# Moving the first heads' operands within SBUF, spreading maxima, and pausing between indirect DMAs in a two-layer attention and mixture-of-experts kernel

## The chip, the cores and the metric

The kernel runs on one core of a Trainium2 chip. Times are device microseconds of one launch. The engines are TensorE (PE, matmuls into the eight PSUM banks `ps`), VectorE (DVE), ScalarE (ACT), GpSimd (POOL) and SyncE (SP, which only issues DMAs). Engines wait for each other through counting semaphores; a DMA adds 16 to one when it has landed. Lower is better.

## The reference

Input `x` has 32 x 32 positions (N = 1024 tokens) and C = 384 channels; there are 12 heads of 32 channels. Everything is float32.

```python
x = x + conv_attention(group_norm(x))        # layer 1: 12 heads, scores + rel_h + rel_w, softmax, projection
t = tokens(x)
t = t + attention(layer_norm(t))             # layer 2: q k^T / sqrt(384), softmax, projection
t = t + moe(layer_norm(t))                   # gate: top 2 of 8 experts, normalized weights
# moe, for each expert e and its tokens:
#   y_e = relu(x @ w1[e].T + b1[e]) @ w2[e].T + b2[e]      hidden size 1536
#   out += weight[token, e] * y_e
```

## The kernel before

In the code L = 0 is layer 1 and L = 1 is layer 2. In layer 2 every factor of the query and key products is split into a high part, which TensorE's fp32r form holds exactly, and a low rest. A product is then three: high by high, low by high, high by low.

**Query and key products.** Six products u = 0 to 5 (queries and keys of three groups of four heads, in turn). Each has two halves of 512 tokens, of nine matmuls each (line 712). u writes the PSUM banks 0 and 1 or 2 and 3 in turn. ScalarE copies each to SBUF (line 1224), and VectorE splits it into the tile `parts`: a high part (line 1019) and a low part (line 1021).

**The way of the operands.** `parts` holds a head's 32 channels on 32 partitions. The later products want three or four blocks of 32 rows one under the other in `qa` and `ka` (97 rows, for the scores) and `qm` and `km` (96 rows, for the maxima). SyncE stores the parts of four heads into the DRAM tensor `heads` (`store_qk`, line 425, eight DMAs of 256 KB for each group), waits until they have landed, and loads `qm` and `km` (`load_m`, lines 437 and 438) and `qa` and `ka` (`load_a`, lines 444 to 447) of head 0 and head 1 (`first_heads`). Then it stores the other two groups, waits again, and loads head 2's. Later heads are loaded one by one.

**Maxima and scores.** For a head's softmax the maximum of each query's scores is needed first. `max_scores` (line 730) makes two matmuls of 96 rows and 512 columns for a query tile, which go round the PSUM banks 0, 1 and 7 (`RING`, `max_bank`). VectorE reduces each to one column (`maximum`, line 1039). A matmul waits until the bank that it writes has been reduced. When eight tiles are through, TensorE turns the column of maxima into a row (`turn_max`, line 735). ScalarE copies it, stores it to DRAM (line 1267) and, when that has landed, loads it as the 97th row of `qa` (line 1273), so that the score product (line 745) already subtracts it. ScalarE takes the exponential (line 1252), `out_product` (line 755) multiplies by the values, and GpSimd adds the first tiles of the sums (lines 597 and 601).

The order of TensorE's work is written out. `BETWEEN[1]` says which (head, query tile) maxima stand at each of the eight value product tiles (line 817): thirteen in all. Where a list has two, the first stands behind the first third. `TURN[1]` says at which value tile ScalarE copies head 0's row; until it has loaded it, it evicts no value tile. Inside `head`, step s makes the scores of key tile s, then maxima of the next head or the one after (`MAXIMA_FIRST` for head 0: head 1's tiles 5, 6 and 7, then head 2's), then output products at s = 1, 3, 5 and 7.

**Routing and experts.** VectorE works out for each token its two experts and the row of `xs` where its normalized row (`tn`) goes. GpSimd scatters them with 16 indirect DMAs of 128 rows, one for each of the two choices r and eight token tiles (line 653). TensorE makes the first tile of 128 rows itself, by 48 products with one-hot matrices (line 915), so that it needs no scatter. SyncE waits for all 16 scatters and loads the second tile (line 532); ScalarE loads the later ones. ScalarE copies each turned tile from PSUM to `xT` (`turned`, line 1325). Ahead of the first it issues two DMAs that spread the rows' places over the partitions, `where<-where` and `where_row<-where` (lines 1328 and 1330), for VectorE's compare (line 1171).

Each row tile then runs 72 products (line 930), ScalarE's relu (line 1343), VectorE's split (lines 1183 and 1185), and 36 split products (line 942). Before the ninth of the twelve hidden groups TensorE turns the next row tile (`turn`, line 908). GpSimd splits the next expert's second weight (`split_expert`, lines 559 and 561).

**The end.** Results of the rows that went to a token's first expert lie in `low`. When SyncE signals (`y_all` at 1) that the tiles of all but the last expert are stored, GpSimd gathers them with eight indirect DMAs (line 663), waits for all eight, multiplies each by the token's weight (line 669) and adds it to `t` (line 672). When the tiles up to the last but one are stored (`y_all` at 2) it gathers the second choice. TensorE and VectorE add the last tile's rows.

## Time and profile before

| | us |
|---|---|
| median of 3 timed runs | 922.0 (921.08 to 925.76) |
| the profiled execution | 930.64 |
| span of that execution | 928.8 |
| TensorE busy | 871.1 (94%) |
| VectorE busy | 486.7 (52%) |
| GpSimd busy | 510.6 (55%) |
| ScalarE busy | 333.0 (36%) |
| mean granted clock of TensorE | 0.97 |

The span is the time from the first to the last instruction of the profiled execution; 1.84 us of its time lie outside. Times of rows are microseconds from the span's start. A busy share of TensorE is no measure of its pace: matmuls are pipelined, and their ends are modelled. Idle time counts where the engine is on the chain that ended last. The granted clock is a share of full speed: 1.00 is 2.4 GHz, 0.50 is 1.2 GHz.

### The profile page before, as it was taken

The numbers are of one execution on the slowest core, as the hardware profiler recorded it, in microseconds if no ns is written. First come the engines' busy times: TensorE is split into PE (matmuls) and PEld (weight loads), VectorE is DVE, ScalarE is ACT, GpSimd is POOL, SyncE is SP. The second block draws the span as 40 slices with busy tenths as digits, with TensorE's granted clock in tenths as the row PEclk, the third lists the DMA queues.
The fourth block names the chain that finished last, engine by engine and source line by source line (L and its number), as shares of the span: only waits on it lengthen the run. The fifth ranks groups of instructions, "written<-read, shape, count | busy, mean of one in ns | idle before, by whom it ended". The sixth has DMA issues, their size and how long they took to land.

```text
span 928.8 us, 18189 instructions
## 1 busy us (share of the span) xinstructions
PE 871.1 (94%) x6200; PEld 662.8 (71%) x6201; DVE 486.7 (52%) x869; ACT 333.0 (36%) x582; POOL 510.6 (55%) x436
## 2 busy tenths in 40 slices
PE   4998999999999889899999998659999999999998
PEld 3475566666665467555555554459999999999997
DVE  5344866776773466677877833624233242233234
ACT  0131254554555222355555662203222232222311
POOL 0300287777875670357676761778357168087383
PEclk9999699999999999799999998769999999999999
DMA  9498523534425009636564426551752644545225
GB/s 300 106 225 257 181 81 94 162 88 118 137 67 167 12 6 227 153 116 196 169 215 145 150 72 206 185 207 35 264 196 93 242 162 148 181 164 189 72 67 158
DMA packets 75073, 139.68 MB, mean 150 GB/s; under 512 B 11576, under 2 KB 49656, under 8 KB 75024
## 3 DMA queue, kind: packets, MB, share of 16 engines
q1 hardware_dynamic: 63424, 120.72, 42.2%
q10 hardware_dynamic: 9552, 12.07, 3.9%
q0 software_dynamic: 2048, 6.29, 2.1%
q8 instruction: 25, 0.41, 0.2%
q14 instruction: 24, 0.20, 0.1%
HBM read 91.82 MB, written 43.55 MB: 146 GB/s over the span
## 4 chain that ended last, share of the span: by engine, by line
PE 83%; DVE 6%; SPq 3%; issue 3%; DMA 2%; ACT 1%; another core or an unknown queue 1%; POOL 1%; ACTq 0%; DVEq 0%; POOLq 0%
PE ps L930 18%; PE ps L755 14%; PE ps L942 13%; PE ps L745 11%; PE ps L730 10%; PE ps L747 5%; PE ps L702 4%; SPq L425 2%; PE ps L861 2%; PE ps L839 2%; DVE mhalf L1039 2%; DMA heads<-parts 1%; PE ps L915 1%; PE ps L817 1%; DMA km<-heads 1%
## 5 line engine op out<-in xcount | busy, mean ns | idle before, releaser
L1039 DVE TENSOR_REDUCE mhalf<-ps 128x1 f32<-128x512 f32 x384 | 240.7, 676 | 92.9 <-PE ps L730 90.9
L1252 ACT ACTIVATE prob<-ps 128x1024 f32<-128x1024 f32 x192 | 192.4, 1025 | 151.8 <-PE ps L747 87.3
L601 POOL TENSOR_TENSOR qf<-qf,prob 128x1024 f32<-128x1024 f32 x76 | 181.3, 2386 | 41.1 <-ACT prob L1252 31.7
L930 PE MATMUL ps<-xT,w 128*128 128x128 f32 x1440 | 166.2, 277 | 8.0 <-issue 6.7
L930 PEld LDWEIGHTS ps<-xT,w 128*128 128x128 f32 x1440 | 165.4, 194 | 8.5 <-issue 8.5
L745 PE MATMUL ps<-qa,ka 97*128 97x512 f32 x384 | 148.1, 429 | 2.9 <-ACT prob L1252 2.0
L730 PE MATMUL ps<-km,qm 96*128 96x512 f32 x384 | 139.1, 440 | 8.6 <-DMA km<-heads 4.5
L1343 ACT ACTIVATE h_f<-ps,b1c 128x128 f32<-128x128 f32 x240 | 68.5, 369 | 148.2 <-PE ps L930 113.7
L559 POOL TENSOR_SCALAR w_hi<-w_raw 128x384 fp32r<-128x384 f32 x96 | 56.1, 584 | 105.2 <-DMA w_raw<-in_w 105.1
L730 PEld LDWEIGHTS ps<-km,qm 96*128 96x128 f32 x384 | 75.2, 197 | 50.9 <-DVE mhalf L1039 31.3
L561 POOL TENSOR_TENSOR w_lo<-w_raw,w_hi 128x384 fp32r<-128x384 f32 x96 | 101.8, 1060 | 8.0
L745 PEld LDWEIGHTS ps<-qa,ka 97*128 97x128 f32 x384 | 69.2, 193 | 49.9 <-issue 19.0
L755 PE MATMUL ps<-prob,va 128*32 128x256 f32 x1536 | 104.1, 386 | 0.0
L597 POOL TENSOR_TENSOR qf<-prob 128x1024 f32<-128x1024 f32 x24 | 57.0, 2376 | 74.9 <-ACT prob L1252 74.9
L1183 DVE CAST h_hi<-h_f 128x512 fp32r<-128x512 f32 x60 | 32.8, 546 | 123.0 <-ACT h_f L1343 119.0
L942 PE MATMUL ps<-w_hi,h_hi 128*128 128x384 f32 x240 | 83.8, 349 | 0.0
L942 PE MATMUL ps<-w_hi,h_lo 128*128 128x384 f32 x240 | 80.5, 336 | 0.0
L942 PE MATMUL ps<-w_lo,h_hi 128*128 128x384 f32 x240 | 80.3, 334 | 0.0
L747 PE MATMUL ps<-qb,eb 128*128 128x512 f32 x192 | 76.9, 401 | 0.0
L755 PEld LDWEIGHTS ps<-prob,va 128*32 128x32 f32 x1536 | 42.8, 110 | 42.6 <-issue 16.7
L1049 DVE RECIPROCAL rec<-vsb 128x64 f32<-128x64 f32 x96 | 49.8, 534 | 42.9 <-ACT vsb L1278 42.9
L618 POOL COPY va<-vf 128x256 f32 (+1 forms) x24 | 9.6, 398 | 96.4 <-DVE vf L1025 56.2
(171 smaller groups left out, 957.7 us busy)
## 6 DMA issues: line engine op xcount, KB each, us to landing
w<-in_w SPq DMA_DIRECT2D x24, 768.0 KB, 7.3
w_raw<-in_w SPq DMA_DIRECT2D x24, 768.0 KB, 11.2
heads<-parts SPq DMA_DIRECT2D x60, 256.0 KB, 4.7
qa<-heads SPq DMA_DIRECT2D x24, 256.0 KB, 3.5
ka<-heads SPq DMA_DIRECT2D x24, 256.0 KB, 3.5
qb<-heads SPq DMA_DIRECT2D x12, 512.0 KB, 5.4
xs<-zero SPq DMA_DIRECT2D x8, 768.0 KB, 4.5
qm<-heads SPq DMA_DIRECT2D x12, 384.0 KB, 5.0
```

The costliest lines, as they stand in the source:

```text
L561: pool.tensor_tensor(w2_lo[b][:, c, :], w2_raw[b][:, c, :], f(w2_hi[b][:, c, :]), ALU.subtract).then_inc(w2_ok[b], 1)
L597: pool.tensor_tensor(acc[b], prob[:, 0, :], prob[:, 1, :], ALU.add).then_inc(a_ok[L], 1)
L601: pool.tensor_tensor(acc[b], acc[b], prob[:, n % NP, :], ALU.add).then_inc(a_ok[L], 1)
L730: mm(max_bank(qt, half), qm[b][0:96, qt * P:(qt + 1) * P], km[b][0:96, half * HALF:(half + 1) * HALF], start=True, stop=True).then_inc(sm_ ...
L745: last = mm(out, ka[b][0:97, s * P:(s + 1) * P], qa[b][0:97, cols], start=True, stop=(L == 1))
L747: last = mm(out, eb[:, s * P:(s + 1) * P], qb[b][:, cols], start=False, stop=True)
L755: last = mm(ps[HD * r:HD * (r + 1), 6, half * QUARTER:(half + 1) * QUARTER], lhs, src[:, r * QUARTER:(r + 1) * QUARTER], start=start, stop ...
L930: last = mm(ps[:, g, c % HG * P:(c % HG + 1) * P], w1[b][:, k, c * P:(c + 1) * P], xT[:, k, :], start=(k == 0), stop=(k == KT - 1))
L942: last = mm(ps[:, 6, 0:C], h[:, c, :], w[:, c, :], start=(c == 0 and n == 0), stop=(c == HC - 1 and n == 2))
L1039: v.tensor_reduce(mhalf[:, b, qt, half:half + 1], max_bank(qt, half), AX.X, ALU.max).then_inc(mx_ok[L], 1)
L1252: act.activation(prob[:, s % NP, :], ps[:, 2 + 2 * (s % 2):4 + 2 * (s % 2), :].rearrange("p a b -> p (a b)"), ACT.Exp).then_inc(p_ok[L], 1)
L1343: last = act.activation(h_f[:, c, :], ps[:, g, c % HG * P:(c % HG + 1) * P], ACT.Relu, bias=b1c[b][:, c:c + 1])
```

## The change

1. *Layer 2, operands.* `qm` and `km` of the first two heads are copied straight from `parts` by DMAs within SBUF (`direct`), four of 128 KB, as soon as u = 0 and 1 are split, ahead of the stores. Behind the first group's stores follow `qa` and `ka`: twelve more, in place of the loads from DRAM. The stores stay. Head 2's `qm` and `km` are loaded behind the second group's stores and not behind the third's.
2. *Layer 2, maxima.* Head 0's query tiles 0 to 3 go among the query and key products (`AMONG`): behind u = 3, behind the first half of u = 4, and behind each half of u = 5. VectorE reduces tiles 0 and 1 behind the split of u = 3, tile 2 behind that of u = 4, tile 3 behind that of u = 5 (`REDUCED`). The products therefore use the banks 2 to 5 in place of 0 to 3 (`qk_bank`), and the value products start at bank 6 (`v_bank`). `BETWEEN[1]` has nine tiles left, and `TURN[1]` goes from value tile 5 to 4.
3. *Routing.* GpSimd waits between the scatters of the two choices until ScalarE has copied the first `xT`. The two DMAs of `where` go from ScalarE's queue to SyncE's.
4. *The end.* Two gathers of the first choice are issued; then, for each tile, GpSimd waits for its gather, multiplies, adds, and issues the gather after next.

```diff
-           ([(0, 0), (0, 1)], [(0, 2)], [(0, 3), (0, 4)], [(0, 5)], [(0, 6), (0, 7)], [(1, 0)], [(1, 1), (1, 2)], [(1, 3), (1, 4)]))
-TURN = (7, 5)
+           ([(0, 4)], [(0, 5)], [(0, 6)], [(0, 7)], [(1, 0)], [(1, 1)], [(1, 2)], [(1, 3), (1, 4)]))
+TURN = (7, 4)
+AMONG = {(3, 1): 0, (4, 0): 1, (5, 0): 2, (5, 1): 3}
+REDUCED = {3: (0, 1), 4: (2,), 5: (3,)}
...
+        def qk_bank(L, u):
+
+            return 2 * L + 2 * (u % 2)
+
+        def v_bank(L, tt):
+
+            return 4 + (tt + 2 * L) % 3
...
+                def direct(h, dst, at, done):
+
+                    sp.dma_start(f(dst), f(parts[h * HD:(h + 1) * HD, 0, at, :])).then_inc(done, 16)
+
+                if L == 1:
+                    sp.wait_ge(split[1], 4)
+                    for h in range(2):
+                        direct(h, qm[h][0:HD, :], 1, ld_m[1][h])
+                        direct(h, km[h][0:HD, :], 2, ld_m[1][h])
                 for m in range(KT):
                     store_qk(m)
                     if m == 0 and L == 1:
+                        for h in range(2):
+                            for i, at in enumerate((0, 1, 1)):
+                                direct(h, qa[h][i * HD:(i + 1) * HD, :], at, ld_a[1][h] if i < 2 else ld_d[h])
+                            for i, at in enumerate((2, 2, 3)):
+                                direct(h, ka[h][i * HD:(i + 1) * HD, :], at, ld_a[1][h] if i < 2 else ld_d[h])
+                    if m == 1 and L == 1:
                         sp.wait_ge(st_q[1][0], 16 * 8)
-                        first_heads()
+                        load_m(2, 0)
...
-            sp.wait_ge(route_ok, 2)
+            sp.wait_ge(route_ok, 3)
+            sp.dma_start(where_dram.rearrange("(p t) -> p t", p=P), where[:, 1, :]).then_inc(ld_l, 16)
+            sp.wait_ge(ld_l, 16)
+            sp.dma_start(where_row[:], where_dram.partition_broadcast(P)).then_inc(ld_l, 16)
             sp.wait_ge(scattered, 16 * 2 * TT)
...
             for r in range(2):
+                if r == 1:
+                    pool.wait_ge(x_ok, 1)
                 for tt in range(TT):
...
+            pool.wait_ge(y_all, 1)
+            for tt in range(2):
+                gather(0, low_dram, where_i[:, 0, tt:tt + 1], tt, gathered[0][tt])
+            for tt in range(TT):
+                pool.wait_ge(gathered[0][tt % 2], 16 * (tt // 2 + 1))
+                pool.tensor_tensor(gy[0][:, tt, :], gy[0][:, tt, :], wts[:, 0, tt:tt + 1].broadcast_to([P, C]), ALU.mult).then_inc(early_ok, 1)
+                pool.wait_ge(early_ok, 2 * tt + 1)
+                pool.tensor_tensor(t[:, tt, :], t[:, tt, :], gy[0][:, tt, :], ALU.add).then_inc(early_ok, 1)
+                if tt + 2 < TT:
+                    gather(0, low_dram, where_i[:, 0, tt + 2:tt + 3], tt + 2, gathered[0][tt % 2])
+            pool.wait_ge(y_all, 2)
+            for tt in range(TT):
+                gather(1, ys_dram, where_g[:, tt:tt + 1], tt, gathered[1][tt])
...
+                        if half == 1:
+                            last.then_inc(qk_mm[L], 1)
+                        if L == 1 and (u, half) in AMONG:
+                            if u == 3:
+                                pe.wait_ge(wide_ok, 4)
+                            max_scores(0, 0, AMONG[u, half])
...
                     v.scalar_tensor_tensor(lo, src, s, f(hi), ALU.mult, ALU.subtract).then_inc(split[L], 1)
+                    for qt in REDUCED.get(u, ()) if L == 1 else ():
+                        maximum(0, 0, qt)
...
-            act.wait_ge(route_ok, 3)
-            act.dma_start(where_dram.rearrange("(p t) -> p t", p=P), where[:, 1, :]).then_inc(ld_l, 16)
-            act.wait_ge(ld_l, 16)
-            act.dma_start(where_row[:], where_dram.partition_broadcast(P)).then_inc(ld_l, 16)
             turned(0)
```

Beside this the value products of layer 2 wait at tile 1 until all six products have been copied, since they share banks 4 and 5; head 0's and head 1's first scores wait for `ld_d` too; and the first choice's gathers have semaphores of their own.

## Rows read from the trace of the kernel before

**Rows 1.** The chain of work that ended last, share of the span by engine.
```profile
PE 83%; DVE 6%; SPq 3%; issue 3%; DMA 2%; ACT 1%; another core or an unknown queue 1%; POOL 1%; ACTq 0%; DVEq 0%; POOLq 0%
```

**Rows 2.** Timeline, TensorE, layer 2's start: start, us, line, operation, tiles, [idle before <-releaser].
```profile
350.47 0.84 PE L712 MATMUL ps<-x_hi,parts 128*128 128x512 f32 x3
...
361.19 0.70 PE L730 MATMUL ps<-km,qm 96*128 96x512 f32 x2 [1.88 <-DMA km<-heads]
...
374.70 0.28 PE L735 MATMUL ps<-ident,mcol 128*8 128x128 f32 x1
...
381.47 0.70 PE L745 MATMUL ps<-qa,ka 97*128 97x512 f32 x2 [0.86 <-DMA qa<-row]
...
388.64 1.22 PE L730 MATMUL ps<-km,qm 96*128 96x512 f32 x2 [2.29 <-DMA km<-heads]
...
393.58 0.75 PE L745 MATMUL ps<-qa,ka 97*128 97x512 f32 x2
```

**Rows 3.** Windows: length, busy PE, PEld, DVE, ACT, POOL, granted clock, DMA share, GB/s.
```profile
383.00:389.00 6.00, 3.52 (x8) 2.32 (x9) 3.38 (x7) 2.27 (x3) 2.74 (x2) 0.54 0.57 145
389.00:394.00 5.00, 5.00 (x25) 2.41 (x25) 2.58 (x4) 1.29 (x2) 4.07 (x2) 0.53 0.01 2
```

**Rows 4.** Timeline, SyncE's queue, layer 2's start.
```profile
346.82 7.89 SPq L425 DMA_DIRECT2D heads<-parts  x8
...
385.44 0.33 SPq L437 DMA_DIRECT2D qm<-heads  x1
```

**Rows 5.** Timeline, TensorE, routing and first row tile.
```profile
606.77 8.14 PE L915 MATMUL ps<-hot,tn 128*128 128x128 f32 x48 [4.97 <-DVEq L1156]
621.59 10.29 PE L930 MATMUL ps<-xT,w 128*128 128x128 f32 x72 [6.67 <-issue]
...
635.88 0.49 PE L908 MATMUL ps<-ident,xs 128*128 128x128 f32 x3
```

**Rows 6.** Timeline, TensorE, last expert.
```profile
884.63 0.49 PE L908 MATMUL ps<-ident,xs 128*128 128x128 f32 x3
...
888.55 8.30 PE L930 MATMUL ps<-xT,w 128*128 128x128 f32 x72 [1.32 <-ACT xT L1325]
```

**Rows 7.** Timeline, ScalarE, routing and last expert.
```profile
620.86 0.49 ACT L1325 ACTIVATE xT<-ps 128x384 f32<-128x384 f32 x1 [24.17 <-remote]
...
887.83 0.49 ACT L1325 ACTIVATE xT<-ps 128x384 f32<-128x384 f32 x1 [5.41 <-remote]
```

**Rows 8.** Timeline, GpSimd, the seventh and the last of the 16 scatters.
```profile
612.95 1.50 POOL L653 DMA_INDIRECT xs<-tn,where_i  x1 [0.30 <-issue]
...
624.89 0.96 POOL L653 DMA_INDIRECT xs<-tn,where_i  x1 [0.31 <-issue]
```

**Rows 9.** Timeline, GpSimd, last expert: last gather, products, sums, first later gather.
```profile
885.28 0.95 POOL L663 DMA_INDIRECT gy<-low,where_i  x1 [0.30 <-issue]
888.44 6.95 POOL L669 TENSOR_TENSOR gy<-gy,wts 128x384 f32<-128x384 f32 x8 [2.22 <-DMA gy<-low,where_i]
895.47 9.65 POOL L672 TENSOR_TENSOR t<-t,gy 128x384 f32<-128x384 f32 x8
906.94 0.99 POOL L663 DMA_INDIRECT tn<-ys,where_g  x1 [1.82 <-SPq L544]
```

**Rows 10.** DMA issues: tiles, engine, count, KB each, median us to landing.
```profile
xnT<-osb SPq DMA_DIRECT2D x92, 32.0 KB, 1.8
...
km<-eb SPq DMA_DIRECT2D x2, 256.0 KB, 4.8
```

**Rows 11.** Timeline, VectorE, layer 2's start.
```profile
352.46 1.22 DVE L1021 SCALAR_TENSOR_TENSOR parts<-prob,parts 128x1024 fp32r<-128x1024 f32 x1
...
361.75 1.28 DVE L1039 TENSOR_REDUCE mhalf<-ps 128x1 f32<-128x512 f32 x2
```

**Rows 12.** Timeline, SyncE's queue, routing.
```profile
628.18 0.33 SPq L532 DMA_DIRECT2D xs<-xs  x1
```

**Rows 13.** Timeline, VectorE, routing.
```profile
613.17 1.16 DVE L1171 TENSOR_SCALAR hot_last<-where_row,last_slot 128x1024 f32<-128x1024 f32 x1 [3.95 <-DMA where_row<-where]
```

More of the change, by code:

```diff
@@ L308, in build_program @@
         zero_st = sem("zero_st")
+        ld_d = [sem(f"ld_d{i}") for i in range(2)]
         early_ok = sem("early_ok")
@@ L326, in build_program @@
         y_all = sem("y_all")
-        gathered = [[sem("gathered0")] * TT, [sem(f"gathered1{i}") for i in range(TT)]]
+        gathered = [[sem(f"gathered0{i}") for i in L2], [sem(f"gathered1{i}") for i in range(TT)]]
         t_out = sem("t_out")
@@ L816, in values @@
                         for k, (x, w) in enumerate(third):
-                            last = mm(ps[:, 4 + tt % 3, 0:C], x, w, start=(n == 0 and k == 0),
+                            last = mm(ps[:, v_bank(L, tt), 0:C], x, w, start=(n == 0 and k == 0),
                                       stop=(n == 2 and k == len(third) - 1))
@@ L1013, in _, with maximum @@
                     v.wait_ge(st_r[1], 16 * (NH - 2))
+                def maximum(h, b, qt):
+                    for half in range(2):
+                        v.wait_ge(sm_ok[L], 2 * (TT * h + qt) + half + 1)
+                        v.tensor_reduce(mhalf[:, b, qt, half:half + 1], max_bank(qt, half), AX.X, ALU.max).then_inc(mx_ok[L], 1)
+                    if qt == TT - 1:
+                        v.wait_ge(mx_ok[L], 2 * TT * (h + 1))
+                        wait(v, mT_ok[L], h - 1)
+                        v.tensor_reduce(mcol[:, b, :], mhalf[:, b], AX.X, ALU.max).then_inc(mc_ok[L], 1)
                 for u in range(2 * KT):
```

89 lines of the change are left out of this document (36 added, 53 removed).

## The prediction

> **What bounds the kernel now.** I read the chain of work that ended last first: TensorE (PE) holds 83% of it, VectorE (DVE) 6%, the issue of SyncE's DMAs 3% [rows 1]. So the time is the work of TensorE plus the places where it stands, and a change that removes no product can win only those places and what TensorE's clock loses beside them. I went through TensorE's timeline for them in the three stretches that the diff touches: the start of layer 2's attention, the routing, and the last expert.
>
> *Layer 2.* Between 350.47 and 381.47 TensorE runs the last query and key products, then the value products with thirteen query tiles of maxima between them. It stands 1.88 us before the first maximum, for `km<-heads`, and 0.86 us before the first score of head 0, for the row of negated maxima. Inside head 0 it stands 2.29 us at 388.64, again for `km<-heads` [rows 2]. The granted clock is 0.54 in 383 to 389 and 0.53 in 389 to 394 [rows 3], that is 1.2 GHz for most of it; the engine had been short of work since 380.6 [rows 2]. The operands come late because SyncE's queue first stores 2 MB to DRAM (8 issues, 7.89 us), waits until they land, and loads them back; head 2's load stands behind 16 more stores and is issued at 385.44 [rows 4].
>
> *Routing.* The 48 gathering products end at 614.91 (606.77 + 8.14), and the first expert product starts at 621.59, 6.67 us later; the 72 products then take 10.29 us [rows 5], where a later tile takes 8.30 [rows 6]. ScalarE's copy `xT<-ps`, which needs nothing but the end of those 48 products, starts at 620.86 [rows 7], 5.9 us after it. In that time GpSimd issues 16 scatters one after the other, until 625.85 [rows 8].
>
> *Last expert.* The same sign again: the three transposes at 884.63 end near 885.1, the copy that needs them starts at 887.83 [rows 6, 7], 2.7 us later, and TensorE stands 1.32 us [rows 6], while GpSimd issues eight gathers (the last one 885.28 to 886.23) [rows 9]. I read both as one thing: what TensorE signals arrives late while GpSimd issues indirect DMAs back to back. The trace shows the delay, not its cause.
>
> **The change part by part.** *Layer 2, the maxima between the query and key products.* Eight matmuls (tiles 0 to 3) move from the value products to behind u = 3, 4 and 5; none is added. 39 products run from 350.47 to 359.31 (361.19 less 1.88), 0.227 us each, so half a product of nine is 2.04 [rows 2]. Tile 0 needs head 0's `qm` and `km` by 350.5. They are issued at 346.8 and 347.2, when the first two splits are done. Copies within SBUF took 1.8 us (32 KB) and 4.8 us (256 KB) to landing [rows 10]; 128 KB between them, 3.3, gives 350.5, in time or up to 1.5 late, and lateness here only eats into the next wait. That wait is new: VectorE's splitting of u = 3 ends at 353.70 (352.46 + 1.22), and a reduction takes 0.64 (1.28 for two) [rows 11]. TensorE is through with tile 0 and half of u = 4 at 352.97, and tile 1's two matmuls reuse banks that come free at 354.34 and 355.0: it stands 1.4 and 0.4. Queued behind it is the other half of u = 4, and so ScalarE's copy and VectorE's split of it. The products then end at 358.63 + 1.84 (eight matmuls) + 1.8 = 362.3. Tile 3 is reduced only after u = 5 is split (about 365.0 to 366.3), so tile 4's second matmul, behind the first value tile, waits to 365.65: 1.6 more. Value tiles 0 to 4 (45 products of 384 columns for 512, 0.17 each, 7.7 us), ten maxima matmuls (2.3) and the wait bring head 0's column to its turn at 374.0, against 374.70 [rows 2]. From turn to first score it took 6.77 us (row stored, loaded back) [rows 2]; TensorE's own remaining work (27 value products 4.6, eight maxima 1.8, the turn 0.2) is as long: 380.8. By the same durations the work from 361.19 to 380.61 before (69 value products, 26 maxima, the turn) would be 17.9, and it took 19.4, so small waits of up to 1.5 come on top. I take 381.5, the start of before: the 1.88 and 0.86 removed return as waits for VectorE, and nothing is won up to here. Setting `TURN` to value tile 4 blocks ScalarE, with value tile 5's eviction behind it, for the row's store; value tile 7 needs only tile 4 evicted, so this costs nothing.
>
> *Layer 2, SyncE's queue.* It gets 16 copies of 128 KB (0.35 to 0.6 each to issue) for 12 loads with 2 MB, so no fewer bytes; but the wait for the landing of the first stores goes. Eight stores pass in 7.89 us [rows 4], 256 KB per us. From 346.8: 0.5 MB copied, 2 MB stored, 1.5 MB copied, 2 MB stored is 6 MB or 24 to 26 us, and head 2's `qm` and `km` are issued near 372, when head 0's maxima are done, ten microseconds before they are needed. If copies whose source is 32 partitions run at half that pace it is 380, still in time. The 2.29 us wait goes whole. What holds TensorE then is VectorE: at 380.8 it has eight reductions of 0.64 left (head 1's tiles 4 to 7) and the short one of the column, so head 2's first maximum ends and the turn of head 1 follows at 386.1; two scores, two maxima and 16 output products (1.9 in all) put the fifth score of head 0 at 388.2, or 388.9 from a start at 381.5. Before it is 393.58 [rows 2]. That is 4.7, if TensorE keeps 2.4 GHz. In the record the clock falls just after 383, when the engine has stood 0.86 us before the first score and is being paced by VectorE; the same stretch is somewhat fuller now, but 353 to 356 and 364 to 367 are emptier. With the fall where it was, only the wait is won: 2.3. Bounds 1.0 (a start at 382.8 and that fall) and 6.0 (at 380.8, and VectorE less in the way); I take 4.7, near the upper end, since most of what was lost there is the wait and the low clock behind it.
>
> *Scatters in halves.* GpSimd issues eight scatters, to 615.71 (612.95 + 1.50, a gap of 0.30, 0.96) [rows 8], and then waits for the copy `xT`. If the late signal comes when issuing stops, or 1.5 us after it (887.83 against 886.23 [rows 7, 9]), `xT` starts at 615.8 to 617.3 and the expert products at 616.5 to 618.0 for 621.59: 3.6 to 5.1. Not all of it stays. The second half now runs from 617.5 to 627.5 (for 625.85), the row tile of the second 128 tokens, issued at 628.18 [rows 12] 2.3 us behind the last scatter, lands at 632.2 or so, and its transposes, at 635.88 before [rows 5], need it: 3.7 is the most that is left. And the clock may be at 1.2 GHz for the first products as now (2.0 us of the 10.29), or the second half may hold the signals of the first tile. Bounds 0 and 4.9; I take 3.0. GpSimd's weight splitting behind the scatters starts 2 us later; expert 1, whose weights it splits, comes two row tiles of some 15 us later. The two DMAs of `where` go from ScalarE's queue to SyncE's, behind expert 1's weights; VectorE's compare, which waits for them, stands at 613.17 [rows 13], and the next that needs VectorE is the first tile's cast behind the first expert products. Nothing, unless they come over 8 us late.
>
> This same compare shows something else: the scatter beside it took 1.50, its neighbours 0.96 [rows 8, 13]. The Trainium skill, "SBUF — State Buffer", section "SBUF: two separate sides", says that GpSimd cannot write an indirect DMA's descriptors while VectorE runs certain two-port operations, so that such a DMA waits for VectorE. This speaks against the change, since the second half now lies beside the first tile's three casts and subtractions. By it the last scatters, and the second row tile behind them, would come some 1.5 us later and the routing would win 1.5 to 2.
>
> *Gathers in turn.* Eight gathers, eight products (6.95) and eight sums (9.65), at 886.2, 895.4 and 905.1 by their ends, become two gathers, then product, sum, gather eight times: 0.87 + 1.21 + 1.25 = 3.3 each for six and 2.1 for two, from about 880.0: to 904.2. The next gathers may start at 906.94 [rows 9], so that 2.7 us cover it; each such microsecond beyond would fall on the end. Never more than two gathers stand in a row before the transposes at 884.63, so the 1.32 us wait goes: 1.3 (0 if a signal is late even behind one gather; 2.0 if the following tile's start is freed as well). The last burst of eight stays as it is.
>
> **The sum.** 4.7 + 3.0 + 1.3 = 9.0. The profiled execution took 930.64 with a span of 928.8, so 921.6 for a like one; the median of the timed runs is 922.0, 8.6 less than the profiled one, and gives **913.0**.
>
> **Rivals.** (1) *The clock takes part of it back, or was not lost in the timed runs.* A second fall of ten microseconds at 1.2 GHz, at the new waits at 353 or 364, costs 5.0: 918.0. If the timed runs of before don't fall at 383 at all (they are 8.6 below the profiled one, which speaks for it), layer 2 wins 1 to 2: 916.2. Against it: the stretch that fell is now fuller. (2) *The second half of the scatters holds the first tile's signals*: the second group of hidden values is signalled at 629.0 (627.5 and 1.5) and TensorE stands in the output products; routing wins nothing: 916.0. For it: a signal is late in both bursts [rows 7]; against: the late ones came after seven and eight issues without a pause, and the first tile's first groups end sooner behind it. (3) *The change does not do what it says*: copies within SBUF, all with source and target on the same 32 partitions, crawl, head 0 waits for `qa`, and layer 2 wins nothing: 917.7. (4) *Slower.* The new waits for VectorE at 353 to 355 and 364 to 366 lower the clock inside the products, where TensorE alone sets the pace, and it stays low to the start of the heads. 38 us at 1.2 GHz cost 19: 922.0 - 9.0 + 19 = 932.0. It decides from 18 us at the low clock on, where half of them passes the gain. Against it: 1.88 us of standing at 359.3 did not lower it [rows 2].
>
> **How the numbers follow.** My forecast 0.50, (1) 0.24, (2) 0.12, (3) 0.06, (4) 0.08. What a measurement of this kernel can tell from no change is some 0.5%, 4.6 us: faster is below 917.4. The forecast, (2) and most of (1) lie there: 0.77; the rest of (1) and (3) within: 0.15; (4) slower: 0.08. The range takes in the low ends of the bounds (6.0 + 4.9 + 2.0 = 12.9, with two more for run to run) and the cases (1) to (3): 907 to 918.5.
>
> **What would show it.** Right: no wait for `km<-heads` in layer 2, waits of 1.4 and 1.6 us for VectorE's reductions between and behind the query and key products, head 0's first score as far from the first product as before and the fifth 4.7 us nearer; `xT` within 2.5 us of the 48 products' end; no idle before the second last tile of the last expert. Wrong: a low granted clock between 350 and 380; expert products that wait in the first tile; sums of GpSimd that end behind the last row tile's store.

## The result and the profile after

| | before | after |
|---|---|---|
| median of 21 timed runs each, us | 924.39 (921.08 to 930.63) | 918.95 (915.79 to 923.66) |
| ratio, 95% interval | | 0.9938 [0.9922, 0.9953] |
| the profiled execution | 930.64 | 921.23 |
| its span | 928.8 | 919.4 |
| mean granted clock of TensorE in it | 0.969 | 0.976 |

The forecast was 913.0, with a range of 907.0 to 918.5. From profile to profile the span fell by 9.4 us, and the sum had said 9.0; but the medians fell by 5.4. The two differ because the profiled execution of before is one of its slowest (four of its 21 runs took 928.7 or more). What that execution had in excess was read as a property of the kernel. Two single runs of the experiments below, one of before_again (2944.28 us) and one of layer2_only (4746.78 us), are far outside all others and are left out of every figure.

The chain that ended last, by engine, is still TensorE's, for [rows 1]:

```profile
PE 85%; DVE 6%; DMA 3%; POOL 2%; issue 2%; ACT 1%; SPq 0%; ACTq 0%; DVEq 0%; POOLq 0%
```

**Layer 2.** Timeline of TensorE, after, for [rows 2] (start, us, line, operation, tiles, idle time before and what ended it). L742 is the maxima, L776 the turn, L788 the scores:

```profile
352.06 0.63 PE L742 MATMUL ps<-km,qm 96*128 96x512 f32 x2
355.92 1.10 PE L742 MATMUL ps<-km,qm 96*128 96x512 f32 x2 [1.15 <-DVE mhalf L1059]
...
367.38 0.50 PE L742 MATMUL ps<-km,qm 96*128 96x512 f32 x1 [1.45 <-DVE mhalf L1059]
...
375.90 0.28 PE L776 MATMUL ps<-ident,mcol 128*8 128x128 f32 x1
...
382.95 0.73 PE L788 MATMUL ps<-qa,ka 97*128 97x512 f32 x2
...
390.51 0.73 PE L788 MATMUL ps<-qa,ka 97*128 97x512 f32 x2
```

352.06 is the place of 350.47 in [rows 2]. From there the first score is 30.89 us away (31.00 before) and the fifth 38.45 (43.11). No wait for `km<-heads` is left, and the two new waits for VectorE are 1.15 and 1.45. The windows at the place of [rows 3] show that the clock no longer falls (columns as there):

```profile
385.00:391.00 6.00, 5.57 (x32) 2.86 (x31) 5.29 (x10) 3.34 (x4) 3.63 (x3) 1.00 0.86 199
391.00:396.00 5.00, 5.00 (x36) 2.96 (x38) 3.79 (x7) 3.50 (x4) 4.64 (x3) 1.00 0.18 53
```

SyncE's queue, after, for [rows 4]: 12 copies within SBUF (the first three stand here), eight stores, and then head 2's load, 24.8 us behind the 352.06, where before it came 35.0 behind the 350.47:

```profile
359.22 3.04 SPq L479 DMA_DIRECT2D qa<-parts  x3
...
368.03 8.74 SPq L436 DMA_DIRECT2D heads<-parts  x8
376.90 1.09 SPq L448 DMA_DIRECT2D qm<-heads  x1
```

**Routing.** TensorE and ScalarE, after, for [rows 5] and [rows 7]:

```profile
602.41 7.79 PE L957 MATMUL ps<-hot,tn 128*128 128x128 f32 x48 [4.97 <-DVEq L1200]
610.24 0.49 ACT L1369 ACTIVATE xT<-ps 128x384 f32<-128x384 f32 x1 [19.52 <-PE ps L957]
610.97 8.30 PE L972 MATMUL ps<-xT,w 128*128 128x128 f32 x72 [0.76 <-ACT xT L1369]
...
626.48 0.55 PE L950 MATMUL ps<-ident,xs 128*128 128x128 f32 x3 [3.02 <-DMA xs<-xs]
```

The copy `xT` starts 0.04 us behind the 48 products, not 5.9. What stands in its place is 3.02 us for the second row tile, which needs all the scatters. GpSimd's scatters and VectorE's steps beside them, after, for [rows 8] and [rows 13]:

```profile
607.32 1.73 POOL L685 DMA_INDIRECT xs<-tn,where_i  x1 [0.30 <-issue]
609.35 0.96 POOL L685 DMA_INDIRECT xs<-tn,where_i  x1 [0.30 <-issue]
610.61 0.96 POOL L685 DMA_INDIRECT xs<-tn,where_i  x1 [0.30 <-issue]
611.88 0.96 POOL L685 DMA_INDIRECT xs<-tn,where_i  x1 [0.31 <-issue]
...
615.67 1.48 POOL L685 DMA_INDIRECT xs<-tn,where_i  x1 [0.30 <-issue]
...
607.04 1.16 DVE L1215 TENSOR_SCALAR hot_last<-where_row,last_slot 128x1024 f32<-128x1024 f32 x1 [2.18 <-DMA where_row<-where]
...
615.63 0.69 DVE L1229 TENSOR_TENSOR h_lo<-h_f,h_hi 128x512 fp32r<-128x512 f32 x1
```

The eighth scatter starts at 610.61 and the ninth at 611.88, 0.31 us behind its end: `xT` was copied by 610.73, so the new wait between the halves holds nothing up. In this execution, which has no late signal, the halves do nothing.

**Last expert.** TensorE, ScalarE and GpSimd, after, for [rows 6], [rows 7] and [rows 9]:

```profile
876.85 0.49 PE L950 MATMUL ps<-ident,xs 128*128 128x128 f32 x3
877.37 0.49 ACT L1369 ACTIVATE xT<-ps 128x384 f32<-128x384 f32 x1 [3.35 <-PE ps L950]
...
893.81 1.00 POOL L703 TENSOR_TENSOR t<-t,gy 128x384 f32<-128x384 f32 x1
897.57 0.99 POOL L692 DMA_INDIRECT tn<-ys,where_g  x1 [2.77 <-SPq L574]
...
906.64 0.49 ACT L1369 ACTIVATE xT<-ps 128x384 f32<-128x384 f32 x1 [3.35 <-PE ps L950]
```

TensorE waits for none of these copies. The one at 906.64 is as prompt as the others, though it lies in the last burst of eight gathers, which the change left as it was. In the first profile of before the copy at that burst was late too, a third one that the prediction didn't see: it starts at 918.48, 2.5 us behind the end of its products, and TensorE doesn't wait for it. So a burst of gathers doesn't of itself delay a signal.

### The profile page after: what moved, and what is told of

Read it like the earlier page. It is cut to its first block, busy times and chain, and to the rows that moved or that the text cites. A ratio compares the mean times of both kernels' runs of the same rounds, so it can differ in the third digit from the quotient of the medians.

```text
span 919.4 us, 18190 instructions
## 1 busy us (share of the span) xinstructions
PE 866.4 (94%) x6200; PEld 660.3 (72%) x6201; DVE 488.2 (53%) x869; ACT 333.0 (36%) x582; POOL 510.4 (56%) x436
## 4 chain that ended last, share of the span: by engine, by line
PE 85%; DVE 6%; DMA 3%; POOL 2%; issue 2%; ACT 1%; SPq 0%; ACTq 0%; DVEq 0%; POOLq 0%
PE ps L972 17%; PE ps L798 14%; PE ps L984 13%; PE ps L788 11%; PE ps L742 10%; PE ps L790 5%; PE ps L755 4%; DVE mhalf L1059 3%; PE ps L765 2%; PE ps L903 2%; PE ps L859 2%; PE ps L881 2%; POOL xs L685 2%; DMA qf<-in_grp 1%; PE ps L950 1%
## 5 line engine op out<-in xcount | busy, mean ns | idle before, releaser
L788 PE MATMUL ps<-qa,ka 97*128 97x512 f32 x384 | 147.0, 425 | 2.2 <-ACT prob L1296 2.0
L742 PE MATMUL ps<-km,qm 96*128 96x512 f32 x384 | 138.4, 435 | 7.8 <-DVE mhalf L1059 5.4
L742 PEld LDWEIGHTS ps<-km,qm 96*128 96x128 f32 x384 | 74.5, 195 | 50.6 <-DVE mhalf L1059 35.0
L788 PEld LDWEIGHTS ps<-qa,ka 97*128 97x128 f32 x384 | 68.8, 191 | 48.4 <-issue 19.9
L1227 DVE CAST h_hi<-h_f 128x512 fp32r<-128x512 f32 x60 | 35.6, 594 | 114.9 <-ACT h_f L1383 114.7
L1093 DVE RECIPROCAL rec<-vsb 128x64 f32<-128x64 f32 x96 | 49.8, 535 | 42.9 <-ACT vsb L1322 42.9
```

The lines of the kernel that those rows point to most:

```text
L742: mm(max_bank(qt, half), qm[b][0:96, qt * P:(qt + 1) * P], km[b][0:96, half * HALF:(half + 1) * HALF], start=True, stop=True).then_inc(sm_ ...
L788: last = mm(out, ka[b][0:97, s * P:(s + 1) * P], qa[b][0:97, cols], start=True, stop=(L == 1))
```

## The experiments

Each is the kernel before or after with the edit shown. The ratio is to the kernel before on the same chip. "Lost" is the mean over its runs of span times (1 - mean granted clock): what the low clock would cost if TensorE had work in all of it. Before had 25.0 to 25.7 of it on the same chips, and after 19.0.

| kernel | median us | ratio, 95% interval | mean clock | lost us |
|---|---|---|---|---|
| before_again | 924.96 | 0.9996 [0.9976, 1.0015] | 0.972 | 25.6 |
| layer2_only | 921.05 | 0.9953 [0.9935, 0.9970] | 0.977 | 21.6 |
| late_parts_only | 924.77 | 1.0004 [0.9985, 1.0023] | 0.972 | 25.9 |
| direct_only | 921.02 | 0.9956 [0.9940, 0.9973] | 0.977 | 21.5 |
| early_only | 921.98 | 0.9959 [0.9943, 0.9975] | 0.976 | 22.2 |
| direct_late | 928.52 | 1.0028 [1.0009, 1.0047] | 0.972 | 26.1 |
| after_late | 925.74 | 1.0011 [0.9997, 1.0025] | 0.975 | 23.4 |
| fill_layer1 | 921.08 | 0.9952 [0.9934, 0.9971] | 0.981 | 17.3 |
| fill_route | 919.84 | 0.9938 [0.9915, 0.9962] | 0.989 | 10.4 |
| early_fills | 919.25 | 0.9937 [0.9922, 0.9953] | 0.995 | 5.0 |
| early_fills_turn10 | 916.64 | 0.9901 [0.9885, 0.9917] | 0.996 | 4.1 |
| after_no_pause | 916.97 | 0.9919 [0.9894, 0.9943] | 0.981 | 17.4 |
| turn10 | 922.10 | 0.9951 [0.9928, 0.9974] | 0.974 | 23.9 |
| half_route_turn10 | 919.52 | 0.9940 [0.9916, 0.9964] | 0.984 | 14.3 |
| half_fills_turn10 | 917.34 | 0.9925 [0.9897, 0.9953] | 0.992 | 7.2 |

### Which part carries the gain

**The kernel before, again**, without an edit.

> The kernel before, unchanged, profiled a second time. Theory A (the profiled execution of before was one of its slow ones: 930.6 against a median of 924.4, and the late signals, 5.9 and 2.7 us behind TensorE's last product in the two bursts, are in such executions only): the new profile shows ScalarE's first xT within 0.3 us of the end of the 48 products and no wait of 1.3 us in the last expert, and takes 922 to 925. Theory B (the signals are late whenever GpSimd issues indirect DMAs back to back): the same two waits again, a time near 930. The clock in head 0 of layer 2: by the theory that the timed runs don't lose it, 1.00 there; by its rival again half for some ten microseconds. Ratio to the kernel before 1.000 by both.

The second profile (924.20) has no late signal. TensorE and ScalarE:

```profile
607.95 8.16 PE L915 MATMUL ps<-hot,tn 128*128 128x128 f32 x48 [4.96 <-DVEq L1156]
616.15 0.49 ACT L1325 ACTIVATE xT<-ps 128x384 f32<-128x384 f32 x1 [18.27 <-PE ps L915]
616.87 8.30 PE L930 MATMUL ps<-xT,w 128*128 128x128 f32 x72 [0.76 <-ACT xT L1325]
...
631.00 0.55 PE L908 MATMUL ps<-ident,xs 128*128 128x128 f32 x3 [1.66 <-DMA xs<-xs]
```

The gap of 6.67 us in [rows 5] is 0.76 here, and the wait of 1.32 in [rows 6] isn't there.

**Parts 3 and 4 alone** (scatters in halves, gathers in turn, `where` on SyncE's queue):

```diff
+                if r == 1:
+                    pool.wait_ge(x_ok, 1)
...
-                    pool.wait_ge(gathered[0][0], 16 * TT)
+                pool.wait_ge(gathered[0][tt % 2], 16 * (tt // 2 + 1))
```

> Only scatters in halves, where on SyncE's queue, and gathers in turn; layer 2 as before. Theory A: no gain in a usual execution, 923 to 925, since the first xT follows its products at once and the second row tile waits for all scatters either way. Theory B: 2.5 to 4 us, 920.5 to 922.

1.0004: they win nothing that can be measured, and the spread is as wide as before (922.26 to 929.44).

**Parts 1 and 2 alone** (after with the other two undone: the reverse of that diff).

> Only the part in layer 2: operands within SBUF, four tiles of maxima among the query and key products; routing and last gathers as before. Theory A (the two late parts win almost nothing in a usual execution): the whole gain of 5.4 us is here, 918 to 920. Theory B (all three parts win their share in every execution, 4.7, 3.0 and 1.3 scaled down alike): 2.5 to 3 us, 921.5. In its profile the fifth score of head 0 starts 38.4 us after the first half of u = 4 by both.

0.9953 is the gain of the change but for 0.15%, within the intervals. The 921.05 us lie above the 918 to 920 that I had expected.

**Part 1 alone** (layer2_only with the maxima back among the value products; `BETWEEN[1]` and `TURN[1]` are as before, too, which the cut doesn't show):

```diff
-AMONG = {(3, 1): 0, (4, 0): 1, (5, 0): 2, (5, 1): 3}
-REDUCED = {3: (0, 1), 4: (2,), 5: (3,)}
+AMONG = {}
+REDUCED = {}
```

> Layer 2's moves within SBUF and the earlier load of head 2, with the maxima where they were before (none among the query and key products) and the late parts as before. If the waits for DMAs (1.88 and 2.29 us) are what counts and the maxima among the products only exchange one wait for another, this is as fast as layer 2's whole part, 918 to 920. If the spread maxima bring something of their own, it is 1 to 2 us slower than that. The waits for km are gone in its profile; before the first score of head 0 there is a wait for the row of maxima of 0.9 to 2.5 us.

0.9956 and 921.02 us, again above the 918 to 920 expected: the maxima among the products add nothing that can be measured to the moves and the load order.

### Moves within SBUF, or the order of the loads

Part 1 holds two edits. I took each alone. **The earlier load in the kernel before:**

```diff
                     if m == 0 and L == 1:
                         sp.wait_ge(st_q[1][0], 16 * 8)
                         first_heads()
+                    if m == 1 and L == 1:
+                        load_m(2, 0)
                 sp.wait_ge(st_q[L][1], 16 * 16)
-                load_m(2, 0)
+                if L == 0:
+                    load_m(2, 0)
```

> The kernel before, with one edit: head 2's operands are loaded behind the second group's stores and not behind the third's. Two theories share the 4 us that the direct moves gave (921.0 for 925.4). Theory K (clock): the gain is the fall of the granted clock in head 0 that no longer comes, and the fall comes from the wait for head 2's operands (2.29 us in one execution of before, 4.37 in another) on top of a stretch paced by VectorE. Then this edit alone does it: no wait for km in head 0, no low clock between 380 and 400, mean granted clock 0.976 to 0.978 where before has a median of 0.972, and 921.0 to 922.0 us. Theory W (the waits of the start): the gain is the earlier first maximum (the wait of 1.7 to 1.9 us for km<-heads at the start of the maxima), which this edit keeps; it then wins 2 us or less, 923.4 or more, at a mean clock of 0.972 to 0.974.

**The moves with the late load** (direct_only, `load_m(2, 0)` behind the third group again):

> Direct moves within SBUF for the first two heads, with head 2's load left behind the third group's stores as in the kernel before. Theory K: since the fall comes from head 2's late operands, the wait for them comes back unless the queue is now far enough ahead; the queue saves the wait for the first landing, so the load is issued a few microseconds earlier, about 380, and lands about 383 to 385: a wait of 0 to 2 us, the clock falls in part of the executions, 922.5 to 924.5 us. Theory W: 921.0 to 921.6 us as with both, since only the start of the maxima counts.

**And after with the late load:**

> The changed kernel with one edit undone: head 2's operands are loaded behind the third group's stores, as before the change. Theory L (the order of the loads): the whole gain of the change is the earlier load of head 2, and the direct copies lengthen SyncE's queue ahead of the late one (it was issued 38.4 us behind the first half of u = 4 with direct copies and 35.0 without). Then this kernel is no faster than before the change, and most likely slower: 926 to 929 us, with a wait of 4 to 6 us for km<-heads in head 0 and a low clock behind it, mean clock 0.971. Theory D (the maxima among the products carry a part of the gain that the earlier load alone doesn't have): 921 to 923.5 us.

The earlier load alone gives 0.9959, as much as all of part 1. The moves without it are slower than before, by 2.6 us. TensorE's and SyncE's rows of direct_late say why:

```profile
367.03 17.72 SPq L436 DMA_DIRECT2D heads<-parts  x16
388.32 0.33 SPq L448 DMA_DIRECT2D qm<-heads  x1
...
391.51 1.22 PE L729 MATMUL ps<-km,qm 96*128 96x512 f32 x2 [5.67 <-DMA km<-heads]
```

Its first half of u = 4 starts at 349.89, so head 2's load is issued 38.4 us behind it, 35.0 in [rows 2, 4]. The 16 copies take 12.3 us of the queue, where the 12 loads and the wait that they replace take 9.9 in the first profile of before, and the 24 stores take 1.3 us longer. The wait for the load becomes 5.67 us. The windows 380 to 400 of before_again, early_only and direct_late, in this order (columns as in [rows 3]):

```profile
380.00:400.00 20.00, 15.20 (x76) 8.81 (x75) 12.46 (x22) 7.80 (x10) 10.23 (x6) 0.83 0.37 95
```

```profile
380.00:400.00 20.00, 19.24 (x117) 11.62 (x115) 16.24 (x28) 10.62 (x13) 10.30 (x6) 1.00 0.60 140
```

```profile
380.00:400.00 20.00, 13.16 (x62) 7.47 (x62) 10.11 (x17) 6.40 (x8) 9.28 (x6) 0.66 0.44 109
```

With the load early TensorE is busy 19.2 of 20 us at the full clock, though early_only still waits 2.02 us for `km<-heads` at the start of the maxima. Its row there, and the fifth score of head 0:

```profile
364.02 0.70 PE L733 MATMUL ps<-km,qm 96*128 96x512 f32 x2 [2.02 <-DMA km<-heads]
...
391.07 0.72 PE L748 MATMUL ps<-qa,ka 97*128 97x512 f32 x2
```

From the first half of u = 4 (353.15) to that score it is 37.9 us, as in direct_only. In the four profiles with layer 2 as before (before, before_again, before_look, late_parts_only) it is 43.0 to 43.4, and 46.6 in direct_late. So what held layer 2 was head 2's load, not the start. In turn10 no load is waited for there, but the clock fell, and it is 40.1; of the 5.2 us or so that the early load wins, by this one profile 2.2 are the low clock's and 3.0 the wait's (an estimate). I had expected 922.5 to 924.5 of direct_late, and it took 928.5. after_late was expected at 926 to 929 and took 925.74, the time of before: with the load late the rest of the change wins nothing.

One thing the moves may still do. In the six profiles that have both edits (after, after_no_pause, layer2_only, direct_only, fill_route, fill_layer1) the clock is 1.00 in 380 to 400. Of the six with the early load alone it fell there in two: 0.83 in turn10, 0.91 in early_fills_turn10. The medians don't tell the two ways apart (0.9956 and 0.9959).

### What is left at the low clock

From before_again to early_only the time went down with what is lost to the clock: 25.6 to 22.2 lost, 925.0 to 922.0 us. So I tried to win the rest in the same way, with products whose result nobody reads where TensorE stands. **Beside the routing, on direct_only:**

```diff
                 if L == 1:
+                    fill({2: 4, 3: 1, 8: 3}.get(tt, 0), ...)
...
+                    fill(13, tn[:, 0, :])
...
             mm(ps[:, 7, 0:(TT + 1) * NE], before[:], taken, start=False, stop=True)
+            for _ in range(11):
+                mm(ps[:, 6, 0:C], ident[:], tn[:, 0, :], start=True, stop=True)
```

> Direct moves with the early load (921.02 us), and beside them products whose result nobody reads, put where TensorE stands in the routing: 8 of 384 columns before three transposes, 13 behind the last gate product, 11 behind the two counting products, each about 0.34 us at full clock and all of them together shorter than the idle time there (5.5 to 6.9 and 5.0 us). Nothing of the computation is left out. Theory K (what varies and what can be won here is the time at the low clock): the fall of 17 us that starts between 587 and 596 doesn't come or is short, the 48 gathering products take 5.2 us in place of 7.7, and the time is 918 to 919.5 with a mean clock of 0.985. Rival R (the clock falls anyway, since the idle stretches remain between the products that were added): the same mean clock of 0.976 to 0.978, the added products run at half speed and stand in the way, 921 to 924 us.

TensorE in fill_route, and its window of the routing (columns as in [rows 3]):

```profile
588.89 8.63 PE L919 MATMUL ps<-tn,ident 128*128 128x384 f32 x26
...
597.76 7.31 PE L947 MATMUL ps<-tn,ident 128*128 128x384 f32 x22
604.90 5.52 PE L961 MATMUL ps<-hot,tn 128*128 128x128 f32 x48
```

```profile
586.00:612.00 26.00, 25.23 (x133) 18.43 (x132) 15.29 (x49) 3.21 (x6) 16.59 (x19) 1.00 0.78 271
```

The same in direct_only:

```profile
599.80 7.71 PE L950 MATMUL ps<-hot,tn 128*128 128x128 f32 x48 [4.96 <-DVEq L1193]
```

```profile
583.00:609.00 26.00, 13.30 (x86) 12.67 (x86) 15.59 (x55) 3.89 (x8) 16.02 (x19) 0.67 0.82 273
```

The clock stays at 1.00 and the gathering products take 5.52 for 7.71; 1.2 us is what is left of it (919.84 against 921.02, with intervals that overlap; 918 to 919.5 was expected). The fills take twice what I gave them (each is two matmuls of 0.33, 26 for 13), so the products start later than they could.

**In layer 1, on direct_only:**

```diff
+                        if L == 0 and m > 0:
+                            for half in range(2):
+                                mm(ps[:, 3, :], qm[h][0:96, m * P:(m + 1) * P],
+                                   km[h][0:96, half * HALF:(half + 1) * HALF], start=True, stop=True)
                         max_scores(h, h, m)
```

> Direct moves with the early load (921.02 us), and beside them two products of 96 rows and 512 columns, whose result nobody reads, ahead of each pair of maxima of layer 1's value products from the second on, where TensorE waits for VectorE's reductions between 83 and 97 us. Nothing of the computation is left out. Theory K: the fall that starts at 93 to 96 us and lasts 10.2 to 17.1 us doesn't come; the maxima stay paced by VectorE (0.64 us each), but the scores behind them run at 0.40 in place of 0.63 us: 918 to 919.5 us, mean clock 0.985. Rival R: the clock falls anyway and the added products at 0.46 us each, with 0.61 for a maximum, are more than VectorE's pace: 921 to 927 us.

921.08, where 918 to 919.5 was expected: nothing won on the median, though 4 us less are lost to the clock (17.3 for 21.5).

**Both, on early_only:**

> The kernel before with head 2's earlier load (921.98 us) and both groups of added products whose result nobody reads: 32 beside the routing and two ahead of each pair of layer 1's maxima. Nothing of the computation is left out. Theory K (low clock with work waiting is what can be won): the routing's fills gave 1.2 us with the direct moves, layer 1's about 0, so 919.5 to 921; if they add up in full as the gathering products' 2.2 us and 1 us of layer 1 say, 918.5. Rival R (a fall avoided here comes back elsewhere): 921.5 to 923 us at a mean clock of 0.978 or less.

919.25. Theory K, by which the low clock that has work waiting can be won back, had said 919.5 to 921, or 918.5 if the parts add up in full; the time lies between the two.

**And the turn two hidden groups later:**

```diff
-TURN_AT = 8
+TURN_AT = 10
```

> The same, with the transposes of the next row tile ahead of the eleventh of the twelve hidden groups and not of the ninth. Two groups take 1.05 us, so TensorE reaches the transposes of the second tile that much later and stands 1.0 us less for the row tile of the scatters (2.4 to 3.1 us as it is), and the fall of 3.4 us behind that wait comes less often: 1 to 2.5 us less than the kernel with the transposes at the ninth. Rival: in each of the 20 other row tiles ScalarE's copy of the turned tile no longer ends inside the two groups that are left (0.49 for three transposes, 0.49 for the copy, of 1.05 us), and each tile waits 0.1 to 0.3 us: 1 to 5 us more.

TensorE around the second row tile, early_fills and then early_fills_turn10:

```profile
624.09 0.90 PE L926 MATMUL ps<-ident,xs 128*128 128x128 f32 x3 [2.50 <-DMA xs<-xs]
...
640.30 0.49 PE L926 MATMUL ps<-ident,xs 128*128 128x128 f32 x3
```

```profile
628.07 0.55 PE L926 MATMUL ps<-ident,xs 128*128 128x128 f32 x3 [1.29 <-DMA xs<-xs]
...
642.77 0.49 PE L926 MATMUL ps<-ident,xs 128*128 128x128 f32 x3
```

From turn to turn it is 16.21 us and 14.70, where a later tile takes 14.63 and 14.64: the later turn costs the others 0.01 us each. After the longer wait the clock fell (0.87 in 624 to 637), after the shorter one it didn't. This kernel, 916.64 us and 0.9901, has the lowest median and ratio of all that were run; its interval ends below that of early_fills, which ran beside it, but not below those of after_no_pause and half_fills_turn10, which ran in another comparison.

**The later turn without fills** (early_only with `TURN_AT = 10`), **and with the routing's fills halved**, without layer 1's and with them:

> The kernel before with head 2's load early (921.98 us) and the transposes of the next row tile ahead of the eleventh hidden group and not of the ninth, with no added products. The wait for the second row tile, 1.6 to 2.4 us, becomes 0.6 to 1.3, and the fall of the clock behind it does not come: 1.0 to 2.5 us less, 919.5 to 921 us, a ratio of 0.993 to 0.9948. Rival: the gain of the later turn needs the full clock in the routing, then 0.9955 or more.

> The same with added products in the routing that are half as many as in the runs before: 7 behind the last gate product (4.6 us, in an idle time of 5.3 to 6.9), 6 behind the counting products (4.0 us of 5.0), 3 and 1 ahead of two transposes; none in layer 1. Theory K: the gathering products run at the full clock (5.5 us) and start 3 to 4 us earlier than with the long fills: 914 to 917 us, mean clock 0.987 or more. Rival: with short idle times left between them the clock falls, and then the time is that of the later turn alone, 919.5 to 921 us, mean clock 0.978.

> The same with layer 1's added products too, which won nothing on direct_only. By that run it takes the time of the kernel without them within 1 us; if the fall of layer 1 is worth its price when nothing else falls, 1 to 3 us less: 912 to 915 us, mean clock 0.995.

turn10 took 922.1 and half_route_turn10 919.5, both above what I expected, and half_fills_turn10 917.3 for 912 to 915. Without fills the later turn wins nothing on the median (0.9951 for 0.9959). The shorter fills did what they should (first expert product 2.6 us earlier than in early_fills_turn10), and it brought nothing. The marks of the profiles say why; times are us from the first projection product, read off each timeline:

| profile | first scatter | scatters take | first expert product | second turn | behind the last scatter | third turn |
|---|---|---|---|---|---|---|
| before [rows 5, 8] | 43.1 | 20.8 | 59.6 | 73.9 | 10.0 | 88.5 |
| before_again | 42.9 | 20.7 | 53.5 | 67.6 | 4.0 | 82.3 |
| after | 41.8 | 21.7 | 52.1 | 67.6 | 4.0 | 83.8 |
| after_no_pause | 41.8 | 20.9 | 52.0 | 66.8 | 4.0 | 81.5 |
| early_fills_turn10 | 42.3 | 20.7 | 52.3 | 67.1 | 4.0 | 81.8 |
| half_route_turn10 | 41.5 | 21.0 | 49.7 | 66.8 | 4.4 | 84.0 |

The second turn comes 4.0 to 4.4 us behind the last scatter, whenever the first expert product started: in all 17 profiles but that of before. So from the first scatter on it is GpSimd's 16 scatters that bound the routing, not TensorE, and what makes TensorE earlier there only makes its wait longer: 3.60 us in half_route_turn10, with a fall of the clock behind it, for 1.29 in early_fills_turn10.

**After without the wait between the halves:**

```diff
-                if r == 1:
-                    pool.wait_ge(x_ok, 1)
```

> The changed kernel without GpSimd's wait between the two halves of the scatters. In its profile that wait held nothing up (the ninth scatter started 0.31 us behind the eighth), so I expect the same time within 0.1%, a ratio to before of 0.993 to 0.996, and a wait for the second row tile between 2.3 and 3.1 us. The rival, that the wait costs something in most executions, gives a ratio of 0.992 or less and a wait of 1.7 us.

0.9919, with 2.33 us of waiting and no fall behind it. The ratio is the one that the rival gave, the wait for the second row tile the one that I expected. The interval holds after's 0.9938, so it isn't shown that the pause costs anything; nor does it win.

**The kernel before once more:**

> The kernel before once more, one profile. Two readings of its first profile differ: late signals of TensorE beside GpSimd's indirect DMAs are in each execution (then the copy xT starts 2.5 to 6 us behind the 48 gathering products' end), or in some only (then it starts within 0.1 us of it, as in the second profile, and the row tile of the second 128 tokens is what is late, by 1.6 us). I expect the second. In both, head 0 waits 2 to 5 us for km<-heads and the clock falls within 6 us of 386.

924.15 us, as expected: `xT` starts at 614.76, 0.04 behind the products, the second row tile is waited for by 1.61 us, head 0 waits 3.44 us for `km<-heads`, and the clock falls at 386.9.

## Why the prediction was wrong, step by step

- **The translation of the sum.** The step that failed: 930.64 less 9.0 is 921.6 (the profile of after took 921.23), and then 8.6 us were taken off again to come to the median. That took the excess of the profiled execution for something that both kernels have. But two terms of the sum, 3.0 for the scatters and 1.3 for the gathers, were priced from that excess, and a run of median length doesn't hold it: late_parts_only, which has these two parts alone, is at 1.0004. Without them, 922.0 less 4.7 is 917.3. Besides, the median of three runs was 922.0, where 21 runs gave 924.39. The forecast is 6.0 us below the 918.95 measured: 4.3 of it are these two terms and 2.4 the median of before, less the 0.7 by which the medians fell by more than 4.7. That the sum of 9.0 came near the 9.4 of the two profiles is no merit of it: 6.4 of the 9.4 are the excess of before's profile over before_again.
- **"What TensorE signals arrives late while GpSimd issues indirect DMAs back to back."** It does in one execution (5.9, 2.7 and 2.5 us late) and in none of the 17 other profiles: there each of the 21 copies `xT` starts 0.04 us behind its products. By the marks that is the whole excess of the first profile over before_again, 6.4 us of span: 6.2 at the third turn, 1.6 behind it, less 1.4 that it was ahead by then. What makes a signal late stays open: no other profile shows one, and the rows of that one name no releaser. ScalarE itself wasn't held up at the first: it had issued `where_row<-where` at 608.79, and the copy is what comes next on it. Nor is it known whether the other slow runs of before had late signals. A time like theirs also comes without: after_late's profile took 929.65 with every copy prompt, and three of late_parts_only's 12 runs took 928.8 or more.
- **Layer 2, 4.7.** In the profiles it is 4.66, with the waits of 1.15 and 1.45 for the 1.4 and 1.6 forecast, and the copies landing after 2.3 to 2.6 us for 3.3. This isn't the first profile's excess: it lost 5.2 us to the clock in 380 to 400 (0.74) where before_again lost 3.4 (0.83), but before_again's wait for the load was 4.37 us for 2.29, and its fifth score came as late (43.4). In timed runs layer2_only is at 0.9953, which is 4.3 us. The forecast had "if TensorE keeps 2.4 GHz" as a condition, and it did: 1.00.
- **"Most of what was lost there is the wait and the low clock behind it."** Right, and more so than I wrote: the load of head 2 alone has the gain. The forecast that the start wins nothing (31.0 us to the first score) held to 0.1 us. The moves within SBUF and the spread maxima, which take most of the working on layer 2, carry nothing of the gain that the runs can show.
- **SyncE's queue.** "16 copies for 12 loads, so no fewer bytes" went by bytes. By the queue's own rows a run of 12 copies takes 8.8 us (359.22 to 367.99), about 0.73 each where the working had 0.35 to 0.6, and head 2's load comes later unless it is also moved. direct_late shows it.
- **Scatters in halves, 3.0.** The row of the second tile was in the working ("3.7 is the most that is left"), as a cap on the gain. It is the bound: without the late signal the second turn hangs on the last scatter alone, so starting the first tile earlier is worth nothing. after's wait of 3.02 us, for 1.66 in before_again, isn't itself lost: TensorE came 1.4 us earlier (52.1 for 53.5) to the same 67.6. But behind it the clock fell (0.90 in 626 to 643, where before_again has 1.00 in 626 to 646), and the third turn comes 16.25 us behind the second, 14.70 in before_again. In that profile being early cost 1.5 us.
- **The scatters' pace.** In after one beside the compare took 1.73 and one beside a split's subtraction 1.48, for 0.96. The Trainium skill, "SBUF — State Buffer", section "SBUF: two separate sides", says that GpSimd can't write descriptors during certain two-port operations of VectorE. The row beside the compare agrees; whether the subtraction is such an operation no run here shows. It is small here: 20.6 to 21.7 us for the 16, with the halves and without.
- **Gathers in turn, 1.3.** From the third turn to the end it is 276.7 us in before_again and in after: they win nothing.
- **Rivals.** None of them held what happened. Rival 1 asked whether the 8.6 us between profile and median could be the clock, and didn't ask whether it could be the late signals. Its other half, that the timed runs don't lose the clock near 383 at all, doesn't hold either: it falls at 388.0 in before_again and at 386.9 in before_look. Rivals 2 and 3 didn't come; nor did rival 4, the clock falling at the new waits (1.00 in 350 to 380, and in 380 to 400).

The Trainium skill, "TensorE: Matmul & The Clock Gate", section "HAM oscillation — how this bites in real kernels", tells of a kernel in which the wait for a DMA between runs of matmuls lets the clock down each time, and advises to order its loop so that TensorE's clock stays up. The trace agrees in part. The wait for head 2's load was 3.4 to 5.7 us in the profiles of before_again, before_look, direct_late and after_late, and in all of them but direct_late the clock fell within it (at 388.0, 386.9 and 389.3). In direct_late and in the first profile of before the clock fell ahead of the wait (at 382.7 and 383.4, where the waits begin at 385.84 and 386.35), and in turn10 and early_fills_turn10 it fell near 387 with no wait for a load. In these four TensorE had stood 0.80 to 1.12 us for the row of maxima before the first score; in layer2_only it stood 0.78 and the clock didn't fall, and in the 13 other profiles 0.64 or less. So the wait for the load isn't all that lets the clock down in this stretch; whether the row's does it was not tested.

## What to carry to other kernels

A profile is one execution. Before a gap of it enters a sum, ask whether the median of the timed runs can contain it. If the profiled time lies above all or most of them, price the gaps that make up the excess at nothing, or the translation to the median counts them twice. Where a queue is serial, ask first which of its loads is waited for, and move that one; a faster way for the others can make it later. Before you make an engine earlier, look what it waits for next.

## What the runs showed of the hardware

- In one execution of 18 profiled, ScalarE's copies started 5.9, 2.7 and 2.5 us behind the TensorE products that they wait for, beside or just behind GpSimd's bursts of indirect DMAs; everywhere else it was 0.04 us. The cause is open.
- Sixteen indirect scatters of 128 rows took 20.6 to 21.7 us of GpSimd, and TensorE's turn of the tile loaded behind them came 4.0 to 4.4 us behind the last (in 17 profiles).
- A copy within SBUF of 128 KB with source and target on 32 partitions lands after 2.3 to 2.6 us in after and 2.6 to 2.9 in direct_late, and takes about 0.6 to 0.73 us of the queue.
- Products without a reader held the granted clock at 1.00 through 26 us of routing in which it was 0.67 without them. But from early_only to early_fills 17 us less were lost (22.2 to 5.0) and some 2 to 3 us of time were won (0.9959 to 0.9937): that low clock lay mostly beside waits for other engines.
